# Moving two stages of the attention output's way through memory, splitting a wait, and cutting loads and stores into tiles

## The chip, the cores and the metric

The kernel runs on one core of one Trainium2 chip. The metric is the device time of one execution in microseconds (us); the shorter the better.

## The reference

x has 2 x 1024 tokens of 512 values. Four residual stages follow each other, each of the form x = x + layernorm(f(layernorm(x))):

```
x = x + _layernorm(_L0_attn_ref(_layernorm(x), w_q, w_k, w_v, w_o))   # 32 heads of 16, full softmax
x = x + _layernorm(_L0_ffn_ref(_layernorm(x), gate, up, down))        # gated FFN, integer weights times scales
x = x + _layernorm(_L1_attn_ref(_layernorm(x), Wqkv, Wo))             # 32 query heads, one key/value head, ALiBi, causal
x = x + _layernorm(_L1_ffn_ref(_layernorm(x), W, b, A, B, p_scores))  # linear plus a clamped low-rank term
```

The change touches the two attention stages only: attention, then the product with w_o (or Wo), its layernorm, and the addition to x.

## The kernel before

Each attention stage (one call of `attention`, tiles named with B and C in the first layer, G and H in the second) computes q, k and v, and then goes through 16 iterations of 4 heads each, 8 for each of the two batches. An iteration is two **turns**, one for each half of 512 queries: 32 turns, 0 to 31. A turn is a row of steps, one for each key tile of 128 (8 in the first layer; 4 or 8 in the causal second). TensorE makes scores and the product with v, ScalarE exponentials, VectorE the maxima of the rows for the turns ahead. The maxima of turn t become rows of the q stack (`max_rows(t)` on SyncE, four small DMAs, L694), and TensorE's first step of turn t waits for them.

The output of a turn goes through DRAM, since heads and their sums have to change partitions. The stages, all but the engines' parts issued by SyncE in the order of its program, are: `copy_o` (PSUM to `o_copy`; VectorE L933 in layer one, ScalarE L890 in layer two), `store_turn` (L701, 256 KB), `fetch` (L712 `o_packed` and L715 `o_sums`), `invert` (VectorE L939), `store_inverse` (L722), `spread_inverse` (L730), and `divide` on GpSimd (L820), which multiplies and writes the tile `on` for two turns of the same half at once. So batch 1's first 512 tokens are complete after the fifteenth multiply, `divide(30)`, and its last 512 after the sixteenth, `divide(31)`. In the middle of the kernel `after_rows(t)`, called behind `max_rows(t)`, issues the stages of turns t-3, t-4, t-6 and t-7; the end has a list of its own.

`Output` takes `on` in 16 tiles of 128 tokens: `tile_high` (ScalarE L1148) and `tile_low` (VectorE L1154) split a tile into two parts, `tile_piece` (TensorE, L74 to L76) makes 12 products of 512 columns, then `tile_stats` (VectorE), `tile_root` (GpSimd L1178), `tile_norm` (VectorE L1171) and `tile_add` (GpSimd L1186, into `xt`). Tiles 0 to 3 run inside the last turns (TILES_AHEAD = 4), tiles 4 to 15 behind them. x comes in and goes out in four blocks of four tiles by `Output.load` (L1112) and `Output.sync` (L1120), 1 MB each, with room for two blocks. w_o is loaded in one DMA (L192) in iteration 1, and GpSimd splits it into parts from turn 3 on (L212, L214). Engines run their programs in order, and a wait holds everything behind it on its engine.

## Time and profile before

| | us |
|---|---|
| median of 3 runs (2146.11 to 2153.83) | 2146.65 |
| the profiled execution's own time | 2145.93 |
| its span | 2144.0 |
| TensorE busy | 1921.5 (90%) |
| VectorE busy | 1422.2 (66%) |
| ScalarE busy | 1142.0 (53%) |

Times inside a trace count from the start of the span. The share of TensorE is an average over stages; in the tail of an attention stage it is far lower. The first attention ends and the gated FFN's first load is issued at 949.65, the second ends at 2018.63.

### The profile page before, as it was taken

To read this page: it belongs to the slowest core of one execution; us is meant where nothing else is said; L and a number is where in the kernel's file an instruction comes from. 1 tells how busy PE (TensorE), PEld (TensorE's weight loads), DVE (VectorE), ACT (ScalarE), POOL (GpSimd) and SP (SyncE) were. 2 spreads that over 40 slices of the span, in tenths; PEclk is the share of its full clock that TensorE was granted. 3 is DMA by queue.
4 is the path that set the end of the run, shared out by engine and by line. 5 is a ranking of instruction groups with operands and counts; after the bars stand their busy time and mean duration, and the time that the engine had idled before them with its cause. 6 is when DMAs were issued, how large, how long until landed. Compare 5 with 4: busy or idle time off the path is not lost. (4 is left out here: it accounts for less than half of the span.)

```text
span 2144.0 us, 31834 instructions
## 1 busy us (share of the span) xinstructions
PE 1921.5 (90%) x11664; PEld 1087.6 (51%) x11664; DVE 1422.2 (66%) x2444; ACT 1142.0 (53%) x2391; POOL 211.3 (10%) x251
## 2 busy tenths in 40 slices
PE   5999999999999999659999999499999999996585
PEld 4864333333333333347888887364444444443463
DVE  5346979999999997354433231567777787763577
ACT  3214777888887887313322221125677777763143
POOL 0000010000000000330010010100100000002313
PEclk9999999999999999879999999699999999998798
DMA  6582443354335431243010100462633444412411
GB/s 202 158 190 74 66 105 69 56 84 76 63 65 82 75 57 39 76 165 100 16 40 1 40 20 0 143 162 68 137 77 79 81 87 90 80 54 76 171 41 59
DMA packets 133434, 178.16 MB, mean 83 GB/s; under 512 B 48244, under 2 KB 59380, under 8 KB 133136
## 3 DMA queue, kind: packets, MB, share of 16 engines
q1 hardware_dynamic: 132896, 175.38, 35.4%
q8 instruction: 92, 1.51, 0.3%
q0 software_dynamic: 384, 0.77, 0.1%
q14 instruction: 62, 0.51, 0.1%
HBM read 111.21 MB, written 64.36 MB: 82 GB/s over the span
## 5 line engine op out<-in xcount | busy, mean ns | idle before, releaser
L927 DVE TENSOR_REDUCE maxesB<-banksB 128x1 f32<-128x1024 f32 x512 | 602.2, 1216 | 92.4 <-PE banksB L993 92.3
L883 ACT ACTIVATE probsB<-banksB 128x512 f32<-128x512 f32 x1024 | 529.6, 602 | 134.8 <-PE banksB L1004 134.7
L924 DVE CUSTOM_DVE_ANT_0 junkG<-banksG,rampG 128x896 bf16<-128x896 f32 (+7 forms) x512 | 368.2, 756 | 104.1 <-PE banksG L993 95.5
L1004 PE MATMUL banksB<-q_stackB,k_stackB 50*128 50x512 f32 x1024 | 405.1, 473 | 7.8 <-DMA q_stackB<-mpartsB 4.8
L883 ACT ACTIVATE probsG<-banksG 128x512 f32<-128x512 f32 (+3 forms) x768 | 326.2, 492 | 119.6 <-PE banksG L1015 68.4
L993 PE MATMUL banksB<-k_stackB,q_stackB 48*128 48x512 f32 x1024 | 345.7, 443 | 3.7
L1004 PEld LDWEIGHTS banksB<-q_stackB,k_stackB 50*128 50x128 f32 x1024 | 167.6, 185 | 270.5 <-ACT probsB L883 228.1
L1004 PE MATMUL banksG<-q_stackG,k_stackG 54*128 54x512 f32 (+3 forms) x768 | 259.6, 413 | 22.0 <-ACT probsG L883 16.5
L1037 PE MATMUL banksB<-probsB,v_onesB 128*32 128x512 f32 x2048 | 276.0, 611 | 0.0
L993 PE MATMUL banksG<-k_stackG,q_stackG 52*128 52x512 f32 (+3 forms) x768 | 248.2, 409 | 11.0 <-DVE maxesG L924 8.2
L993 PEld LDWEIGHTS banksB<-k_stackB,q_stackB 48*128 48x128 f32 x1024 | 155.0, 186 | 85.0 <-DVE maxesB L927 73.8
L1004 PEld LDWEIGHTS banksG<-q_stackG,k_stackG 54*128 54x128 f32 x768 | 126.9, 186 | 103.8 <-ACT probsG L883 75.2
L993 PEld LDWEIGHTS banksG<-k_stackG,q_stackG 52*128 52x128 f32 x768 | 126.2, 187 | 96.6 <-DVE maxesG L924 62.8
L1332 DVE SCALAR_TENSOR_TENSOR hD<-u_psD,suD,siluD 128x512 f32<-128x512 f32 (+1 forms) x44 | 33.0, 750 | 202.3 <-PE u_psD L76 199.9
L1037 PE MATMUL banksG<-probsG,v_onesG 128*32 128x512 f32 (+3 forms) x1536 | 165.4, 503 | 0.1
L1015 PE MATMUL banksG<-masks,halves 64*128 64x64 bf16 (+1 forms) x1024 | 119.9, 211 | 0.0
L1292 ACT ACTIVATE siluD<-g_psD,sgD 128x512 f32<-128x512 f32 (+1 forms) x44 | 30.3, 688 | 132.1 <-PE g_psD L76 132.0
L1300 ACT ACTIVATE hhD<-hD 128x512 fp32r<-128x512 f32 (+1 forms) x44 | 27.8, 632 | 118.3 <-DVE hD L1332 118.3
L1037 PEld LDWEIGHTS banksB<-probsB,v_onesB 128*32 128x32 f32 x2048 | 40.4, 108 | 63.7 <-ACT probsB L883 35.1
L74 PE MATMUL g_psD<-xhTD,wg_highD 128*128 128x512 f32 (+1 forms) x176 | 70.3, 399 | 1.4 <-DVE xlTD L171 1.4
L76 PE MATMUL g_psD<-xhTD,wg_lowD 128*128 128x512 f32 (+1 forms) x176 | 70.3, 399 | 0.0
L74 PE MATMUL y_psD<-wd_highD,hhD 128*128 128x512 f32 (+1 forms) x176 | 70.0, 398 | 0.0
(229 smaller groups left out, 2759.5 us busy)
## 6 DMA issues: line engine op xcount, KB each, us to landing
q_stackB<-q_parts SPq DMA_DIRECT2D x96, 128.0 KB, 6.8
k_stackB<-k_parts SPq DMA_DIRECT2D x96, 128.0 KB, 7.2
q_stackG<-q_parts SPq DMA_DIRECT2D x96, 128.0 KB
q_parts<-partsA SPq DMA_DIRECT2D x16, 512.0 KB, 4.2
k_parts<-partsA SPq DMA_DIRECT2D x16, 512.0 KB, 2.8
turns<-o_copyB SPq DMA_DIRECT2D x32, 256.0 KB
q_parts<-partsF SPq DMA_DIRECT2D x16, 512.0 KB, 2.8
turns<-o_copyG SPq DMA_DIRECT2D x32, 256.0 KB, 3.3
```

The costliest lines, as they stand in the source:

```text
L74: pe.matmul(out, left[0], right[0], start=start, stop=False)
L76: return pe.matmul(out, left[1], right[0], start=False, stop=stop)
L883: act.activation(probs[:, (i % ring) * GH + h, first:HALF], st_ps[:, n % n_st, first:HALF], ACT.Exp).then_inc(st_used, 1)
L924: dve.tensor_tensor_reduce(junk[:, n % JUNK, 0:width], scores, ramp[:, SEQ - width:SEQ], 1.0, LOWEST, ALU.add, ALU.max, out).then_inc(maxe ...
L927: dve.reduce_max(out, scores, AX.X).then_inc(maxed, 1)
L993: ins = pe.matmul(s_ps[:, slot_of[n] + part, 0:b - a], qst[at, it % 3, half, h % GS, qt * P:(qt + 1) * P], kst[at, it % 3, h % kh, a:b], s ...
L1004: ins = pe.matmul(st_ps[:, n % n_st, first:HALF], kst[at, it % 3, h % kh, kt * P:(kt + 1) * P], qst[at, it % 3, half, h % GS, first:HALF], ...
L1015: ins = pe.matmul(st_ps[:, n % n_st, first:first + wide], halves[at, a, :], masks[at, a, 0:wide], start=False, stop=a == 1)
L1037: ins = pe.matmul(o_ps[32 * h:32 * h + 32, first:HALF], vone[:, it % 2, kt, h % vh, :], probs[:, (i % ring) * GH + h, first:HALF], start=k ...
L1292: act.activation(silu[0:k, :], g_ps[0:k, :], ACT.Silu, scale=sg[0:k, j:j + 1]).then_inc(silu_out, 1)
L1300: act.activation(hh[0:k, c % 2, :], h[0:k, :], ACT.Copy).then_inc(hh_out, 1)
L1332: dve.scalar_tensor_tensor(out=h[0:k, :], in0=u_ps[0:k, :], scalar=su[0:k, j:j + 1], in1=silu[0:k, :], op0=ALU.mult, op1=ALU.mult).then_in ...
```

## The change

Six edits. (1) `after_rows(t)` issues the stages of turns t-2, t-3, t-4 and t-5 instead of t-3, t-4, t-6 and t-7, and VectorE's `invert` goes with them. (2) The list at the end is written anew: the last turns' stages stand earlier, and `store_turn(31)` comes behind three stores of single tiles instead of behind block 0's store and block 2's load. (3) `tile_high` for block 2 waits for fifteen multiplies, and for block 3 for sixteen (before, both for sixteen); `tile_low(12)` takes the place in the order that `tile_low(8)` had. (4) x is loaded and stored a tile (256 KB) at a time through eight slots, one load in each of the iterations 1 to 8. (5) w_o is loaded in four chunks in iterations 1 to 4, and GpSimd splits them from turn 10 on. (6) `divide(31)` and `invert(31)` stand later among the tiles, the multiplies of turns 26 and 27 earlier.

```
--- before.py
+++ after.py
@@ -191,6 +191,13 @@
         for k, ap in self.aps.items():
             sp.dma_start(self.raw[k][:, :, :], ap.rearrange("(c p) e -> p c e", p=P)).then_inc(self.loaded[k], 16)
+    def load_chunk(self, sp, c):
+        k = self.order[0]
+        if c:
+            sp.wait_ge(self.loaded[k], 16 * c)
+        sp.dma_start(self.raw[k][:, c, :], self.aps[k][P * c:P * (c + 1), :]).then_inc(self.loaded[k], 16)
     def split_high(self, act, keys):
         for k in keys:
             act.wait_ge(self.loaded[k], 16)
@@ -207,8 +214,7 @@
     def split_piece(self, pool, i):
         k = self.order[0]
-        if i == 0:
-            pool.wait_ge(self.loaded[k], 16)
+        pool.wait_ge(self.loaded[k], 16 * (i + 1))
         pool.tensor_copy(self.high[k][:, i, :], self.raw[k][:, i, :]).then_inc(self.high_out, 1)
         pool.wait_ge(self.high_out, i + 1)
         pool.tensor_tensor(self.low[k][:, i, :], self.raw[k][:, i, :], self.high[k][:, i, :].bitcast(F32),
@@ -732,14 +738,14 @@
             def after_rows(t):
-                if 0 <= t - 3 < TURNS:
-                    store_turn(t - 3)
-                if 0 <= t - 4 < TURNS:
-                    fetch(t - 4)
-                if 0 <= t - 6 < TURNS:
-                    store_inverse(t - 6)
-                if 0 <= t - 7 < TURNS:
-                    spread_inverse(t - 7)
+                if t >= 2:
+                    store_turn(t - 2)
+                if t >= 3:
+                    fetch(t - 3)
+                if t >= 4:
+                    store_inverse(t - 4)
+                if t >= 5:
+                    spread_inverse(t - 5)
             def load_more():
                 sp.wait_ge(proj.w.ready, proj.w.total)
@@ -775,29 +781,36 @@
                     load_stacks(sp, it + 2)
                 if it == 1:
                     proj.stored_block(sp, NB - 1)
-                    out.w.load(sp)
-                    out.load(sp, 0)
-                    sp.wait_ge(out.x_loaded, 16)
-                    out.load(sp, 1)
-            store_turn(last - 2)
-            fetch(last - 3)
+                if 1 <= it <= DC:
+                    out.w.load_chunk(sp, it - 1)
+                if 1 <= it <= out.SLOTS:
+                    out.load(sp, it - 1)
             fetch(last - 2)
-            spread_inverse(last - 6)
-            store_inverse(last - 5)
-            spread_inverse(last - 5)
+            spread_inverse(last - 4)
+            store_inverse(last - 3)
             store_turn(last - 1)
+            spread_inverse(last - 3)
             fetch(last - 1)
-            for t in range(last - 4, last):
-                store_inverse(t)
-                spread_inverse(t)
-            out.sync(sp, range(0, 1))
+            store_inverse(last - 2)
+            spread_inverse(last - 2)
+            store_inverse(last - 1)
+            spread_inverse(last - 1)
+            early = max(tiles_ahead - 1, 0)
+            for t in range(early):
+                out.store(sp, t)
             store_turn(last)
             fetch(last)
+            for t in range(early):
+                out.load(sp, out.SLOTS + t)
             store_inverse(last)
             spread_inverse(last)
+            for t in range(early, NT):
+                out.store(sp, t)
+                if early <= t - 1 < NT - out.SLOTS:
+                    out.load(sp, out.SLOTS + t - 1)
             sp.wait_ge(m_rows, n_rows * TURNS)
             sp.wait_ge(i_spread, 16 * TURNS)
-            out.sync(sp, range(1, NB))
+            sp.wait_ge(out.stored, 16 * NT)
         @block.gpsimd
         def _(pool):
@@ -823,8 +836,8 @@
             def after_split(t):
                 if t >= 8 and t // 2 % 2:
                     divide(t - 8)
-                if 3 <= t < 3 + out.w.count("wo"):
-                    out.w.split_piece(pool, t - 3)
+                if 10 <= t < 10 + out.w.count("wo"):
+                    out.w.split_piece(pool, t - 10)
             for dst, src in copies:
                 pool.dma_start(dst, src).then_inc(copied, 16)
@@ -851,12 +864,11 @@
                 if tile_at(i, 2) is not None:
                     out.tile_root(pool, tile_at(i, 2))
                     out.tile_add(pool, tile_at(i, 2))
-                if i == first_of[last] + 5:
-                    divide(last - 5)
-                    divide(last - 4)
+                if i in (first_of[last] + 1, first_of[last] + 3):
+                    divide(last - 5 + (i - first_of[last] - 1) // 2)
             divide(last - 1)
             for t in range(tiles_ahead, NT):
-                if t == tiles_ahead + 2:
+                if t == tiles_ahead + 4:
                     divide(last)
                 out.tile_root(pool, t)
                 out.tile_add(pool, t)
@@ -952,13 +964,12 @@
             for i, (it, half, kt, *_) in enumerate(steps):
                 for n in units_at[i]:
                     maximum(n)
-                if i - 1 == first_of[2 * it + half] and 2 * it + half >= 5:
-                    invert(2 * it + half - 5)
+                if i - 1 == first_of[2 * it + half] and 2 * it + half >= 3:
+                    invert(2 * it + half - 3)
                 if not causal and kt == 0 and i:
                     copy_o(2 * it + half - 1)
-                if i - first_of[last] in (2, 4):
-                    invert(last - 4 + (i - first_of[last] - 2))
-                    invert(last - 3 + (i - first_of[last] - 2))
+                if i - first_of[last] in (3, 5):
+                    invert(last - 2 + (i - first_of[last] - 3) // 2)
                 if tile_at(i, -1) is not None:
                     out.tile_low(dve, tile_at(i, -1))
                 if tile_at(i, 2) is not None:
@@ -969,13 +980,13 @@
                 copy_o(TURNS - 1)
             for t in range(tiles_ahead, NT):
                 out.tile_stats(dve, t, s_ps)
-                if t + 2 < NT and (t + 2) % (NT // BATCH):
+                if t + 2 < NT and t + 2 != NT - TB:
                     out.tile_low(dve, t + 2)
                 if t > tiles_ahead:
                     out.tile_norm(dve, t - 1, s_ps)
-                if t + 2 < NT and (t + 2) % (NT // BATCH) == 0:
+                if t + 2 == NT - TB:
                     out.tile_low(dve, t + 2)
-                if t == tiles_ahead + 1:
+                if t == tiles_ahead + 2:
                     invert(last)
             out.tile_norm(dve, NT - 1, s_ps)
...
+    SLOTS = 8
     def __init__(self, sb, load_sb, sems, tag, x, x_out, wo_ap, power):
         self.x, self.x_out, self.power = x, x_out, power
...
-        self.xt = load_sb(f"xt{tag}", [P, 2, TB, D], F32)
+        self.xt = load_sb(f"xt{tag}", [P, self.SLOTS, D], F32)
...
-    def load(self, sp, nb):
-        sp.dma_start(self.xt[:, nb % 2, :, :], self.x[BLK * nb:BLK * (nb + 1), :].rearrange("(t p) d -> p t d", p=P)
-                     ).then_inc(self.x_loaded, 16)
-    def sync(self, sp, blocks):
-        for nb in blocks:
-            sp.wait_ge(self.added, TB * (nb + 1))
-            if nb:
-                sp.wait_ge(self.stored, 16 * nb)
-            sp.dma_start(self.x_out[BLK * nb:BLK * (nb + 1), :].rearrange("(t p) d -> p t d", p=P), self.xt[:, nb % 2, :, :]
-                         ).then_inc(self.stored, 16)
-            if nb + 2 < NB:
-                sp.wait_ge(self.stored, 16 * (nb + 1))
-                sp.wait_ge(self.x_loaded, 16 * (nb + 2))
-                self.load(sp, nb + 2)
-            if nb == NB - 1:
-                sp.wait_ge(self.stored, 16 * NB)
+    def load(self, sp, t):
+        if t:
+            sp.wait_ge(self.x_loaded, 16 * t)
+        if t >= self.SLOTS:
+            sp.wait_ge(self.stored, 16 * (t - self.SLOTS + 1))
+        sp.dma_start(self.xt[:, t % self.SLOTS, :], self.x[P * t:P * (t + 1), :]).then_inc(self.x_loaded, 16)
+    def store(self, sp, t):
+        sp.wait_ge(self.added, t + 1)
+        if t:
+            sp.wait_ge(self.stored, 16 * t)
+        sp.dma_start(self.x_out[P * t:P * (t + 1), :], self.xt[:, t % self.SLOTS, :]).then_inc(self.stored, 16)
     def tile_piece(self, pe, t, c, y_ps):
@@ -1141,8 +1149,10 @@
     def tile_high(self, act, t, divided, turns):
-        if t % (NT // BATCH) == 0:
-            act.wait_ge(divided, turns * (t // (NT // BATCH) + 1))
+        batch, half = divmod(t // TB, 2)
+        if t % TB == 0:
+            act.wait_ge(divided, turns * (batch + 1) - 1 + half)
         if t >= 3:
             act.wait_ge(self.made, t - 2)
         act.activation(self.onh[:, t % 3, :, :], self.on[:, :, t * P:(t + 1) * P], ACT.Copy).then_inc(self.high_out, 1)
@@ -1180,9 +1190,8 @@
     def tile_add(self, pool, t):
         pool.wait_ge(self.normed, t + 1)
-        if t % TB == 0:
-            pool.wait_ge(self.x_loaded, 16 * (t // TB + 1))
-        x = self.xt[:, t // TB % 2, t % TB, :]
+        pool.wait_ge(self.x_loaded, 16 * (t + 1))
+        x = self.xt[:, t % self.SLOTS, :]
         pool.tensor_tensor(x, x, self.yn[:, t % 2, :], ALU.add).then_inc(self.added, 1)
```

SyncE in the first layer, behind the stacks of iteration 3 (`q_stackB`, `k_stackB`). Before:

```order
L675 DMA q_stackB<-q_parts 16x4x512
L676 DMA k_stackB<-k_parts 16x2x1024
L192 DMA wo_rawC<-in_w_o 128x4x512
L1112 DMA xtC<-in_x 128x4x512 x2
L694 DMA q_stackB<-mpartsB 1x8x128 x4
L684 DMA v_loadB<-v_rows 128x512
```

Now:

```order
L681 DMA q_stackB<-q_parts 16x4x512
L682 DMA k_stackB<-k_parts 16x2x1024
L199 DMA wo_rawC<-in_w_o 128x512
L1129 DMA xtC<-in_x 128x512
L700 DMA q_stackB<-mpartsB 1x8x128 x4
L690 DMA v_loadB<-v_rows 128x512
```

The maxima's rows (L694, now L700) stood behind two loads of 1 MB, of which the second waited for the first; now they stand behind two of 256 KB with no wait between.

SyncE at the end of the first layer's attention, from the last but one inverse's spreading on, with the semaphores waited for. Before:

```order
L730 DMA o_inverseB<-inverses 64x1x512 [waits inverses_spread_1,inverses_stored_1]
L1120 DMA x<-xtC 128x4x512 [waits x_added_C_1]
L1112 DMA xtC<-in_x 128x4x512 [waits x_loaded_C_1,x_stored_C_1]
L701 DMA turns<-o_copyB 128x512 [waits o_stored_1,o_copied_1]
L712 DMA o_packedB<-turns 64x1x512 [waits o_moved_1,sums_moved_1,o_divided_1,o_stored_1]
L715 DMA o_sumsB<-turns 128x1x16 [waits sums_inverted_1]
L722 DMA inverses<-o_recipB 128x16 [waits inverses_stored_1,sums_inverted_1]
```

Now:

```order
L736 DMA o_inverseB<-inverses 64x1x512 [waits inverses_spread_1,inverses_stored_1]
L1135 DMA x<-xtC 128x512 [waits x_added_C_1]
L1135 DMA x<-xtC 128x512 [waits x_stored_C_1,x_added_C_1] x2
L707 DMA turns<-o_copyB 128x512 [waits o_stored_1,o_copied_1]
L718 DMA o_packedB<-turns 64x1x512 [waits o_moved_1,sums_moved_1,o_divided_1,o_stored_1]
L721 DMA o_sumsB<-turns 128x1x16 [waits sums_inverted_1]
L1129 DMA xtC<-in_x 128x512 [waits x_stored_C_1,x_loaded_C_1] x3
L728 DMA inverses<-o_recipB 128x16 [waits inverses_stored_1,sums_inverted_1]
L736 DMA o_inverseB<-inverses 64x1x512 [waits inverses_spread_1,inverses_stored_1]
L1135 DMA x<-xtC 128x512 [waits x_stored_C_1,x_added_C_1] x2
```

The last turn's store no longer follows a 1 MB store and load; three loads of a tile stand between its sums and its inverses, and every store of a tile but the first waits for the one before.

GpSimd at the same place, from tile 3's addition on. Before:

```order
L1186 TENSOR_TENSOR xtC<-xtC,ynC 128x512
L820 TENSOR_TENSOR onC<-o_packedB,o_inverseB 128x512
L1178 TENSOR_TENSOR yrstdC<-ymvC,power 128x1
L1186 TENSOR_TENSOR xtC<-xtC,ynC 128x512
L1178 TENSOR_TENSOR yrstdC<-ymvC,power 128x1
L1186 TENSOR_TENSOR xtC<-xtC,ynC 128x512
L820 TENSOR_TENSOR onC<-o_packedB,o_inverseB 128x512
```

The second L820 is the last turn's multiply, behind tile 5; now it stands behind tile 7, with two more pairs of root and addition ahead of it (its row in the new order, between tiles 7 and 8):

```order
L1195 TENSOR_TENSOR xtC<-xtC,ynC 128x512
L833 TENSOR_TENSOR onC<-o_packedB,o_inverseB 128x512
L1188 TENSOR_TENSOR yrstdC<-ymvC,power 128x1
L1195 TENSOR_TENSOR xtC<-xtC,ynC 128x512
L1188 TENSOR_TENSOR yrstdC<-ymvC,power 128x1
```

## Rows read from the trace of the kernel before

**Rows 1.** PE, timeline, three stretches: start, us, form, idle before and its releaser.

```profile
279.79 0.79 PE L1004 MATMUL banksB<-q_stackB,k_stackB 50*128 50x512 f32 x1 [4.44 <-DMA q_stackB<-mpartsB]
...
911.03 0.79 PE L74 MATMUL banksB<-wo_highC,onhTC 128*128 128x512 f32 x1 [18.72 <-DVE onlTC L1154]
```

**Rows 2.** SyncE, timeline, at the loads of x in iteration 1 of each layer.

```profile
260.74 13.29 SPq L1112 DMA_DIRECT2D xtC<-in_x  x2
...
1510.92 10.45 SPq L1112 DMA_DIRECT2D xtH<-x  x2
```

**Rows 3.** GpSimd, timeline, first layer: w_o's first split, the last turn's multiply.

```profile
271.04 0.62 POOL L212 CAST wo_highC<-wo_rawC 128x512 fp32r<-128x512 f32 x1 [20.87 <-DMA wo_rawC<-in_w_o]
...
908.32 1.26 POOL L820 TENSOR_TENSOR onC<-o_packedB,o_inverseB 128x512 f32<-128x512 f32 x1 [2.62 <-DMA o_inverseB<-inverses]
```

**Rows 4.** VectorE, timeline, first layer: a turn's output copied, one row a turn.

```profile
257.32 0.68 DVE L933 COPY o_copyB<-banksB 128x512 f32<-128x512 f32 x1
...
306.69 0.68 DVE L933 COPY o_copyB<-banksB 128x512 f32<-128x512 f32 x1
...
327.72 0.68 DVE L933 COPY o_copyB<-banksB 128x512 f32<-128x512 f32 x1
```

**Rows 5.** ScalarE, timeline, second layer: outputs of turns 1, 5, 7 and 31 copied.

```profile
1498.08 0.60 ACT L890 ACTIVATE o_copyG<-banksG 128x512 f32<-128x512 f32 x1
...
1561.69 0.60 ACT L890 ACTIVATE o_copyG<-banksG 128x512 f32<-128x512 f32 x1
...
1591.25 0.60 ACT L890 ACTIVATE o_copyG<-banksG 128x512 f32<-128x512 f32 x1
...
1955.09 0.60 ACT L890 ACTIVATE o_copyG<-banksG 128x512 f32<-128x512 f32 x1 [1.18 <-PE banksG L1037]
```

**Rows 6.** SyncE, timeline, both tails: last turn's store, inverses, next stage's load.

```profile
892.31 0.45 SPq L701 DMA_DIRECT2D turns<-o_copyB  x1
...
902.69 0.33 SPq L722 DMA_DIRECT2D inverses<-o_recipB  x1
904.90 0.53 SPq L730 DMA_DIRECT2D o_inverseB<-inverses  x1
...
949.65 0.36 SPq L108 DMA_DIRECT2D xD<-x  x1
...
1962.49 0.46 SPq L701 DMA_DIRECT2D turns<-o_copyG  x1
...
2018.63 0.36 SPq L108 DMA_DIRECT2D xI<-x  x1
```

**Rows 7.** VectorE, timeline, first tail: last copy, tile 7's low part, norms of 8 and 15.

```profile
881.97 0.68 DVE L933 COPY o_copyB<-banksB 128x512 f32<-128x512 f32 x1
...
887.93 0.69 DVE L1154 TENSOR_TENSOR onlTC<-onC,onhTC 128x512 fp32r<-128x512 f32 x1
...
921.12 0.81 DVE L1171 TENSOR_SCALAR ynC<-banksB,ymvC,yrstdC 128x512 f32<-128x512 f32 x1 [0.44 <-POOL yrstdC L1178]
...
941.94 0.81 DVE L1171 TENSOR_SCALAR ynC<-banksB,ymvC,yrstdC 128x512 f32<-128x512 f32 x1 [1.89 <-POOL yrstdC L1178]
```

**Rows 8.** DMA issues of the whole span: count, size, median us to landing.

```profile
v_loadB<-v_rows SPq DMA_DIRECT2D x16, 256.0 KB, 3.0
...
x<-xtH SPq DMA_DIRECT2D x4, 1024.0 KB, 4.3
...
x<-xD SPq DMA_DIRECT2D x4, 256.0 KB, 2.0
```

**Rows 9.** The tile view of turns: landing times of its stores and fetches.

```profile
DMA to landing us min/median/max: 2.0/3.3/5.9
```

**Rows 10.** Timeline, first layer, mid run: sums fetched on SyncE.

```profile
639.84 0.55 SPq L715 DMA_DIRECT2D o_sumsB<-turns  x1
```

**Rows 11.** Timeline, first layer, mid run: VectorE's reciprocal of that turn's slot.

```profile
646.51 0.24 DVE L939 RECIPROCAL o_recipB<-o_sumsB 128x16 f32<-128x16 f32 x1
```

**Rows 12.** Windows: us, busy us by engine, granted clock (PEclk), DMA share, GB/s.

```profile
278.00:282.00 4.00, 2.21 (x9) 1.45 (x10) 0.92 (x1) 1.38 (x3) 0.00 (x0) 0.50 0.61 177
```

## The prediction

> **What bounds the kernel now.** I read the timeline of TensorE first, looking for its long gaps, then the engine behind each gap, then SyncE, whose program order decides both. In the middle of the attention stages TensorE is nearly full; nothing that the change moves can shorten that. Two kinds of place are different, and each occurs once per attention layer.
>
> The first is iteration 1. TensorE waits 4.44 us at 279.79 for the maxima's rows [rows 1], and right after it the granted clock is 0.50, the lower level of 1.2 GHz [rows 12]. The rows came late because SyncE stood between two 1 MB loads of x for 13.29 us, in the second layer 10.45 [rows 2]; GpSimd, which has to split the maximum too, was itself standing before w_o's first split until 271.04 [rows 3]. What it cost in all is read from the copies of a turn's output, one a turn. First layer: 257.32 to 306.69 are two turns in 49.37 us, and the next turn takes 327.72 - 306.69 = 21.03 [rows 4]; 49.37 - 2 x 21.03 = **7.3 us** lost. Second layer: four turns from 1498.08 to 1561.69 in 63.61, two regular ones 29.56 (1561.69 to 1591.25) [rows 5]; 63.61 - 59.12 = **4.5 us** lost.
>
> The second is the tail. TensorE idles 18.72 us before tile 8 at 911.03 [rows 1], since the last turn's output goes through DRAM: its copy starts at 881.97 [rows 7], but SyncE issues the store at 892.31 [rows 6], having stood behind block 0's store and block 2's load; the inverses are spread at 904.90, and GpSimd multiplies at 908.32 [rows 3, 6]. From then on tiles run at VectorE's and GpSimd's pace, tile 8's norm at 921.12 to tile 15's at 941.94: seven steps, 2.97 us each [rows 7]. The next stage's load is issued 949.65 - 941.94 = 7.7 us after that [rows 6, 7].
>
> **The change part by part.**
>
> *Iteration 1.* SyncE no longer waits between loads there, and GpSimd's splits come when the chunks have long landed. SyncE issues two DMAs more in iterations 1 to 4, one more to 8; these stand behind the stacks' loads, ahead of maxima that are not due yet, so I cost them at nothing. With the rows on time TensorE has no gap there and no low clock: both losses go, 7.3 + 4.5 = **11.8 us**. Bounds: 0 (if the rows were late for the traffic's sake) and 11.8.
>
> *Two turns sooner, in mid run.* The same DMAs, so no time by itself. What gets tighter is the reciprocal: its sums are now those that SyncE has fetched in the same turn. The place of the two in a turn stays, and that is 646.51 - 639.84 = 6.7 us from issue to use [rows 10, 11]. Landings of this tile are 2.0 to 5.9, median 3.3 [rows 9]: covered. If not, VectorE stands, with the maxima behind it and TensorE's next turn behind those. At the end the gain is that turns 28 to 30 are through before the last turn ends.
>
> *The tail, first layer.* (a) The last store goes out when the copy is done, 881.97 + 0.68, say 882.7, instead of 892.31: the three tiles' stores ahead of it belong to tiles 0 to 2, done in the turn. (b) It lands after 3.3 [rows 9], the fetches go out at about 886 and 886.6, and three loads of tiles follow, each waiting for the one before: 3.0 us for 256 KB [rows 8], so 887.1, 890.1, 893.1. These hold the inverses' store to 893.5; spread 904.90 - 902.69 = 2.2 later [rows 6], 895.7, and landed 3.4 later (908.32 - 904.90 [rows 3, 6]), 899.1. (c) Meanwhile TensorE makes tiles 4 to 11 without the gap, since turn 30's multiply is done at about 882. Tile 7's low part at 887.93 [rows 7] is followed by tile 4's norm at about 888.7 (before, GpSimd stood in a multiply there). Eleven steps of 2.97 to tile 15 are 32.7; the last turn's multiply adds its 1.3 [rows 3] between tiles 7 and 8, where it no longer waits (tile 7 is added after 899.1); and tile 12's parts, which can only be made behind that multiply and stand behind tile 9's norm, I take at 1 us. So tile 15's norm comes at 888.7 + 32.7 + 1.3 + 1 = 923.7, its addition ends 2.1 later, and by computing alone the last store goes out at **925.9**. TensorE stands up to 4 us before tile 12 and may fall to the lower clock, as it did after 4.44 us [rows 1, 12]; that adds up to 2 here.
>
> (d) But the stores are a chain of their own: 13 of them behind the last spreading, each waiting for the one before. The first, tile 3's, goes out at 896.3. A store of 256 KB lands in 2.0 [rows 8], 2.2 with issue; five of them have a load behind them, and I take 3.3 for such a round (the load's 3.0 and an issue). Twelve steps: 2.3 + 5 x 3.3 + 6 x 2.2 = 32.0, so the last goes out at **928.3**, later than by computing. The stores thus end last, by 2.4 us, and hide a fall of the clock.
>
> (e) The last landing is of 256 KB, 2.0, not of 1 MB, 4.3 [rows 8]. Before, 7.7 lay between tile 15's norm and the next stage; less 2.1 for the norm and the addition and 4.3 for the landing leaves 1.3 for the barrier. So the next stage begins at 928.3 + 2.0 + 1.3 = 931.6 instead of 949.65: **18.1 us**.
>
> *The tail, second layer.* The last copy is at 1955.09, so the store goes out at 1955.8 instead of 1962.49 [rows 5, 6]. That is 1073.1 after the first layer's; with the same chain the next stage begins at 931.6 + 1073.1 = 2004.7 instead of 2018.63 [rows 6]: **13.9 us**.
>
> Sum: 11.8 + 18.1 + 13.9 = 43.8. The profiled execution took 2145.93 (span 2144.0), 0.7 below the median of the runs, so 2145.9 - 43.8 = 2102.1 against the profiled one and 2102.9 against the median; **2103 us**.
>
> **A price that the trace bounds only from far: the chain of small stores.** No stores of 256 KB that wait for each other stand in the trace. The four in the FFN overlap and land in 2.0; the widest landing near is 5.9 [rows 8, 9]. I take 2.2 and 3.3, nearer to the first, since in the tail nothing else moves but the loads. The Trainium skill ("DMA: Bandwidth & Descriptors", section Bandwidth) advises to batch DMAs to 1 MiB or more, which speaks against this edit; its section on the anatomy of a DMA fits a fixed 2.0 us plus bytes at 436 GB/s. By that a tile's store is 2.6 us, twelve steps 31.2, and the total about 1.6 us lower than mine; the trace agrees on the fixed part, since a block of four times the size takes 2.3 us more, not four times as long.
>
> **The rivals.**
>
> *The forecast (72%)*: both holes of iteration 1 go, both tails shorten by 14 to 20 us, stores or computing ending last.
>
> *The chain of stores binds harder (16%)*. For it: SyncE's program has them all behind the last spreading, and landings of 3.3 are the median of a tile of this size beside other traffic [rows 9]. With 4.3 in the five rounds with a load and 3.3 in the seven without, the twelve steps are 44.6 instead of 32.0, 12.6 later in each layer: 2128. Against it: in the tail the queues are nearly empty. Part of the way is likelier than all of it.
>
> *The holes of iteration 1 remain (4%)*, because the stacks' loads and not SyncE's wait make the rows late: only the tails gain, 32.0, and the time is 2115. Against it: the same stacks' loads stand in every iteration, and the regular turns have no such gap.
>
> *Computing binds (5%)*: landings of 2.0 all over and tile 12 never late; each tail 2.4 to 4 us shorter than forecast, 2096.
>
> *Slower (2%)*: the reciprocal waits in mid run. Each turn in which the sums land later than 6.7 us after issue [rows 10, 11] holds VectorE by the difference. To eat 43.8 us over some 58 turns takes 0.75 each, a landing of 7.5; beyond 7.7 the kernel is slower by over 0.5%, and at 8.5 it stands at 2103 + 58 x 1.8 = 2207. Against it: 5.9 is the longest landing seen [rows 9].
>
> *Nothing moves (1%)*: something that the trace does not show releases tile 8 and the maxima's rows.
>
> **How the numbers follow.** Half a per cent, 11 us, is about what a measurement of this kernel can tell from no change. The forecast case spans 2096 to 2109; the range reaches up into the chain of stores half way (2116) and down past the case in which computing binds (2094), which leaves out what is beyond half of that rival and the last two. **Range 2094 to 2116.** Faster by over 0.5% (below 2136): all of the forecast, of computing, of the remaining holes and nearly all of the chain, 96%; within, 2%; slower, 2%.
>
> **What the new profile would show.** Right: no wait of TensorE on `q_stackB<-mpartsB` above a few tenths at 275 to 280, copies of turns 21.0 apart throughout; the last `turns` store within 1 us of the last copy; TensorE's longest gap in the tail before tile 12, some 4 us; 13 stores of `xt` in a row on SyncE, about 2.2 apart and 3.3 with loads; the FFN's first load about 7.3 + 18.1 = 25.4 us earlier, at 924, and the adapter's first load 43.8 earlier, at 1975. Wrong: reciprocals waiting for `o_sums` in mid run, stores more than 4 us apart, additions waiting for x's tiles, or a gap before tile 8.

## The result, and the profile after

The changed kernel takes 2114.5 us (median of 4 runs, 2109.6 to 2119.3) beside 2146.4 for the kernel before on the same chip: ratio 0.985, interval 0.9823 to 0.9877. The forecast was 2103 and the range 2094 to 2116, so the direction is right and the median lies near the upper end. The profiled execution took 2118.06, with a span of 2116.2; it is 3.6 above the median, so a part of what its stretches show belongs to this one execution.

The span splits into stretches between rows that stand in both traces (turn copies, and the next stage's first load):

| stretch | before | after | difference | forecast |
|---|---|---|---|---|
| start to turn 0's copy, layer one | 215.26 | 214.47 | -0.8 | 0 |
| turn 0's to turn 31's copy, layer one | 666.71 | 669.83 | **+3.1** | -7.3 |
| tail, layer one | 67.68 | 47.93 | **-19.75** | -18.1 |
| gated FFN and projection | 528.44 | 529.88 | +1.4 | 0 |
| turn 0's to turn 31's copy, layer two | 477.00 | 476.24 | -0.8 | -4.5 |
| tail, layer two | 63.54 | 48.65 | **-14.9** | -13.9 |
| adapter stage | 125.4 | 129.2 | +3.8 | 0 |

The tails gave what was forecast and a little more. In the first layer, turns behind iteration 1 took back more than iteration 1 gave. TensorE's timeline of the changed kernel shows where (it answers to [rows 1]):

```profile
318.72 0.50 PE L1015 MATMUL banksB<-q_stackB,k_stackB 50*128 50x512 f32 x1 [1.96 <-DMA q_stackB<-mpartsB]
...
407.60 0.50 PE L1015 MATMUL banksB<-q_stackB,k_stackB 50*128 50x512 f32 x1 [1.68 <-DMA q_stackB<-mpartsB]
...
909.57 0.50 PE L74 MATMUL banksB<-wo_highC,onhTC 128*128 128x512 f32 x1 [2.78 <-DVE onlTC L1164]
```

The wait at 279.79 is gone, but the same releaser, the maxima's rows, now holds TensorE twice, with the rows that SyncE issues in its iterations 2 and 4. VectorE's copies of turns 4 and 5 (as in [rows 4]) and the last one:

```profile
298.73 0.68 DVE L945 COPY o_copyB<-banksB 128x512 f32<-128x512 f32 x1
322.63 0.69 DVE L945 COPY o_copyB<-banksB 128x512 f32<-128x512 f32 x1 [0.74 <-PE banksB L1048]
...
884.30 0.69 DVE L945 COPY o_copyB<-banksB 128x512 f32<-128x512 f32 x1 [1.84 <-PE banksB L1048]
```

This turn took 322.63 - 298.73 = 23.90 instead of 21.04. The eight turns to the copy of turn 12 lose 9.8 us in all. SyncE's timeline, from the last stack load of iteration 2 on:

```profile
304.41 0.59 SPq L682 DMA_DIRECT2D k_stackB<-k_parts  x1
305.04 0.42 SPq L199 DMA_DIRECT2D wo_rawC<-in_w_o  x1
305.50 0.43 SPq L1129 DMA_DIRECT2D xtC<-in_x  x1
311.93 2.79 SPq L700 DMA_DIRECT2D q_stackB<-mpartsB  x4
```

SyncE is free and issues the rows at 311.93, 21 us after the last ones (290.89): nothing on SyncE is late. The windows (columns as in [rows 12]) show what is:

```profile
302.00:306.00 4.00, 4.00 (x28) 1.29 (x26) 3.76 (x4) 3.46 (x7) 0.00 (x0) 1.00 1.06 117
306.00:310.00 4.00, 4.00 (x28) 1.66 (x24) 3.50 (x4) 2.92 (x7) 0.00 (x0) 1.00 1.08 125
310.00:314.00 4.00, 4.00 (x28) 1.39 (x27) 3.56 (x4) 3.69 (x9) 0.45 (x1) 1.00 1.05 124
...
320.00:324.00 4.00, 4.00 (x18) 1.57 (x17) 2.79 (x4) 2.01 (x5) 0.61 (x1) 0.50 0.12 39
```

The DMA engines are full (share 1.05 to 1.08) from 302 to 314, at only 117 to 125 GB/s, and the rows stand behind that. Behind the late rows the granted clock falls to 0.50 (1.2 GHz). The waits before these two rows are 3.6 us of the 9.8, so the turns behind them lose more than the waits. The kernel before had the same full stretch behind its stacks, without these loads, and then a gap before its rows, which it issued at 319.90:

```profile
314.00:318.00 4.00, 4.00 (x28) 1.70 (x24) 3.50 (x4) 2.92 (x7) 0.00 (x0) 1.00 1.00 116
318.00:322.00 4.00, 4.00 (x27) 1.36 (x27) 3.56 (x4) 3.69 (x9) 1.80 (x3) 1.00 0.12 19
```

In the tail, SyncE (as [rows 6]), then VectorE's statistics of tile 12, its last norm, and GpSimd's last addition:

```profile
885.02 0.32 SPq L707 DMA_DIRECT2D turns<-o_copyB  x1
...
888.26 7.19 SPq L1129 DMA_DIRECT2D xtC<-in_x  x3
895.64 0.33 SPq L728 DMA_DIRECT2D inverses<-o_recipB  x1
898.06 0.54 SPq L736 DMA_DIRECT2D o_inverseB<-inverses  x1
...
915.01 14.21 SPq L1135 DMA_DIRECT2D x<-xtC  x7
...
932.23 0.37 SPq L108 DMA_DIRECT2D xD<-x  x1
```

```profile
914.22 0.70 DVE L1169 BATCH_NORM_STATS2 ystatsC<-banksB 128x6 f32<-128x512 f32 x1 [1.77 <-PE banksB L76]
...
926.73 0.81 DVE L1181 TENSOR_SCALAR ynC<-banksB,ymvC,yrstdC 128x512 f32<-128x512 f32 x1 [1.88 <-POOL yrstdC L1188]
```

```profile
927.62 1.26 POOL L1195 TENSOR_TENSOR xtC<-xtC,ynC 128x512 f32<-128x512 f32 x1 [0.92 <-DVE ynC L1181]
```

The last addition ends at 928.88, and the seventh store of the last row is issued at 915.01 + 14.21 - 0.32 = 928.90, as soon as its tile is there; in the second layer the two times are 1983.10 and 1983.13. So computing ends last and not the chain of stores, but in the first layer only just. A narrower window shows the store before the last alone:

```profile
926.71 0.32 SPq L1135 DMA_DIRECT2D x<-xtC  x1
```

Tile 14's addition had ended at 926.19, so this store still waited for the one before it. Stores that wait only for each other stand 2.06 apart here (922.59, 924.64, 926.71), and by that the chain alone would have reached the last store at 928.8, an estimate, 0.1 us before the addition's end. TensorE's wait of 2.78 us at 909.57 reaches the tail: the clock behind it is 0.57 in the mean,

```profile
910.00:914.00 4.00, 4.00 (x12) 3.15 (x11) 1.94 (x5) 0.00 (x0) 3.08 (x4) 0.57 0.66 222
```

and VectorE waits 1.77 us for tile 12's product at 914.22.

### The profile page after: what moved, and what is told of

Same layout as the page of the kernel before. It is cut to its first block and busy times, and to the rows that moved or that the text cites. A ratio compares the mean times of both kernels' runs of the same rounds, so it can differ in the third digit from the quotient of the medians.

```text
span 2116.2 us, 31952 instructions
## 1 busy us (share of the span) xinstructions
PE 1929.8 (91%) x11664; PEld 1092.3 (52%) x11664; DVE 1420.7 (67%) x2444; ACT 1141.4 (54%) x2391; POOL 211.2 (10%) x251
## 5 line engine op out<-in xcount | busy, mean ns | idle before, releaser
L826 POOL TENSOR_TENSOR mpartsB<-mrowB,mpartsB 16x128 fp32r<-16x128 f32 x32 | 14.4, 451 | 571.6 <-ACT mrowB L885 571.6
```

## The experiments

Three groups: what makes turns long in mid run (e1, e2, e3, e4), what the parts of the tail are worth (e3, e6, e7), and what bounds the tail now (e5, e8, e9, e10). The profiled execution of each is cut as in the table above; ratios are to the kernel before on the same chip.

**e1_idle.** The loads of iterations 1 to 8 move from behind the stacks to behind the even turn's stages, ahead of a stretch in which the DMA engines have nothing to do (share 0.00 from 324 to 334):

```
                 if 2 * it not in early_turns:
                     after_rows(2 * it)
+                if it == 1:
+                    proj.stored_block(sp, NB - 1)
+                if 1 <= it <= DC:
+                    out.w.load_chunk(sp, it - 1)
+                if 1 <= it <= out.SLOTS:
+                    out.load(sp, it - 1)
```

> The changed kernel, with the loads of iterations 1 to 8 (a chunk of w_o and a tile of x) issued behind the stages of the even turn instead of behind the stacks. Theory (the loads share the DMA engines with the stacks and make the maxima's rows late): in the first layer the 318.72 and 407.60 waits for q_stackB<-mpartsB go and so does the low clock behind them, the copies of turns 4 to 12 are 21.04 to 21.1 apart, and the time from turn 0's copy to turn 31's falls from 669.8 by 8 to 10 us to about 660; the second layer by 0 to 4; ratio to before 0.9805, about 2105 us. Rival (the shift of the stages by two turns or the clock by itself makes the long turns): the long turns stay at 23 to 24 us, the ratio stays at 0.985.

Measured: 2102.85 us, ratio 0.9771 (0.9744 to 0.9799). Copies 4 to 11 are 21.02 to 21.05 apart, first to last copy 661.8 (was 669.8), second layer 472.4 (was 476.2), tails unchanged (47.3 and 48.7). The same windows of this kernel:

```profile
306.00:310.00 4.00, 4.00 (x28) 1.66 (x24) 3.51 (x4) 2.93 (x7) 0.00 (x0) 1.00 1.07 125
310.00:314.00 4.00, 4.00 (x28) 1.39 (x27) 3.56 (x4) 3.69 (x9) 0.45 (x1) 1.00 0.34 46
```

The rows are again issued at 311.93, but now the engines have just come free (0.34). Later there is one wait of 0.81 us for rows at 739.47, with no load of x near: the stacks alone leave hardly any slack. The ratio fell by more than these 8.0 us, by 17 from 0.985. The spans differ by 3.9 in the second layer's turns and by 4.5 in the FFN and the adapter, which the edit doesn't touch. The same edit between e5 and e8, on one chip, takes the median from 2109.0 to 2101.0: 8.0 us is what it is worth.

**e2_apart.** x's tiles are loaded in iterations 5 to 12, so 256 KB an iteration instead of 512:

```
-                if 1 <= it <= out.SLOTS:
-                    out.load(sp, it - 1)
+                if DC < it <= DC + out.SLOTS:
+                    out.load(sp, it - 1 - DC)
```

> The changed kernel, with the tiles of x loaded in iterations 5 to 12 instead of 1 to 8, so that behind the stacks of iterations 1 to 4 stand 256 KB instead of 512. Theory (DMA engines are full behind the stacks): the two waits for the maxima's rows shrink from 1.96 and 1.68 us to a few tenths or nothing, turns 4 to 12 lose under 2 us instead of about 9, and the time is 2107 us. Rival (stage shift or clock): turns as long as before the edit, 2114 us. If already 256 KB more were too much, iterations 5 to 12 would show holes too.

Measured: 2109.7 us, ratio 0.9807 (0.9779 to 0.9835). Turns 4 to 12 lose 0.2 us, but later turns, with the x tiles, lose some 4 in all, with this wait behind the second of those tiles:

```profile
485.07 0.50 PE L1015 MATMUL banksB<-q_stackB,k_stackB 50*128 50x512 f32 x1 [1.10 <-DMA q_stackB<-mpartsB]
```

So 256 KB behind the stacks is at the edge: nothing in iterations 1 to 4, then now and then 1 us with its low clock.

**e3_lags.** The stages' shift by two turns is undone, with the old list at the end and the old places of the reciprocals and multiplies there:

```
-                if t >= 2:
-                    store_turn(t - 2)
-                if t >= 3:
-                    fetch(t - 3)
+                if t >= 3:
+                    store_turn(t - 3)
+                if t >= 4:
+                    fetch(t - 4)
...
-                if i - 1 == first_of[2 * it + half] and 2 * it + half >= 3:
-                    invert(2 * it + half - 3)
+                if i - 1 == first_of[2 * it + half] and 2 * it + half >= 5:
+                    invert(2 * it + half - 5)
```

> The changed kernel, with the stages of a turn's output issued as before the change (for turns t-3, t-4, t-6 and t-7, the reciprocal five turns behind) and the old order of the last turns' stages; loads by tile and chunk, the split wait and the tail stay. Theory (extra loads behind the stacks): the waits of 1.96 and 1.68 us and the long turns stay, 670 us from the first to the last copy of layer one; the tail of layer one is up to 3 us longer, since turns 28 to 30 come later; about 2116 us. Rival (the shift by two turns makes the rows late): the long turns go, about 661 us from copy to copy, and the time is about 2107.

Measured: 2127.1 us, ratio 0.9884 (0.9858 to 0.991). Long turns stay, though not the same ones, with 670.1 from copy to copy and a wait of 1.91 at 361.70, so the shift doesn't cause them. The tails are 56.4 and 55.4, longer by 8.5 and 6.7 where I expected up to 3. SyncE:

```profile
883.93 0.41 SPq L728 DMA_DIRECT2D inverses<-o_recipB  x1
887.18 0.53 SPq L736 DMA_DIRECT2D o_inverseB<-inverses  x1
887.77 6.79 SPq L1138 DMA_DIRECT2D x<-xtC  x3
894.65 0.38 SPq L707 DMA_DIRECT2D turns<-o_copyB  x1
```

The last copy is at 884.60, but the last turn's store goes out ten us later: the old list's inverses and the three stores behind them are still being issued. The shift and the new list together clear SyncE before the last turn ends; no run parts the two.

**e4_wait.** SyncE waits again, with the traffic unchanged:

```
                 if 1 <= it <= out.SLOTS:
                     out.load(sp, it - 1)
+                if it == 1:
+                    sp.wait_ge(out.x_loaded, 16)
```

> The changed kernel, and SyncE waits in iteration 1 for the first tile of x to land (same traffic, only SyncE's wait is back). Theory (a wait of SyncE holds the rows behind it): the landing took 12.4 us in the first layer, rows that were issued at about 269.9 go out at about 273.7 to 276, TensorE waits 2 to 6 us at about 278 and falls to the lower clock, so the first layer is 3 to 7 us longer than the changed kernel's; in the second layer 0 to 4; in all 2118 to 2124 us. Rival (the traffic alone made the hole of iteration 1 before the change, and SyncE's wait cost nothing): no hole there and 2114 us.

Measured: 2123.0 us, ratio 0.987 (0.9838 to 0.9902). The rows go out at 273.69, and TensorE stands:

```profile
277.65 0.79 PE L1017 MATMUL banksB<-q_stackB,k_stackB 50*128 50x512 f32 x1 [2.46 <-DMA q_stackB<-mpartsB]
```

The second layer's hole is back as well: a wait of 2.51 at 1520.62 and one turn of 24.30 instead of 19.98 (24.15 in the kernel before). First to last copy is 673.8 and 478.8, 4.0 and 2.6 above the changed kernel. The two turns to the copy of turn 4 lose 5.8 us, where they lost 7.3 before the change. So SyncE's wait alone makes most of the old hole, as the prediction had it, and the traffic behind the stacks is a second cause. A further 3.0 us of this run lie in the FFN and projection, which the edit doesn't touch.

**e5_order.** In the tail, the loads of tiles 8 to 10 come behind the inverses' spreading, the last reciprocal and multiply one tile sooner, tile 12's low part ahead of tile 9's norm:

```
             store_inverse(last)
             spread_inverse(last)
             for t in range(early, NT):
+                if t - early < NT - out.SLOTS:
+                    out.load(sp, out.SLOTS + t - early)
                 out.store(sp, t)
...
-                if t == tiles_ahead + 4:
+                if t == tiles_ahead + 3:
                     divide(last)
```

> The changed kernel with the tail in another order: the loads of tiles 8 to 10 come behind the inverses' spreading, one ahead of each store, the last reciprocal and the last multiply stand one tile sooner, and tile 12's low part ahead of tile 9's norm. Theory (computing ends last, and TensorE's wait before tile 12 with the low clock behind it is what delays it): the wait of 2.78 us at 909.57 shrinks to below 1 us, the last store comes 3 to 4 us sooner after the last copy in each layer (tails of 47.9 and 48.7 us become about 44.5 and 45), the kernel is 6 to 8 us faster than the changed one: ratio to before 0.982 where the changed one had 0.985. Rival (the chain of stores ends last, as the prediction had it): the loads now stand among the stores, the tails stay at 48 us or grow by up to 3, ratio 0.985 to 0.988.

Measured: 2109.0 us, ratio 0.9818 (0.9799 to 0.9837), which is not told apart from 0.985. TensorE's wait before tile 12 halves to 1.38 us, yet the tails are 47.6 and 48.1, only 0.4 and 0.5 shorter. The theory misses. The rival has the tails' number (48) but not the cause: the last store goes out at 927.76, as the last addition ends (927.73). GpSimd's timeline shows what sets the pace:

```profile
912.01 1.30 POOL L1191 TENSOR_TENSOR xtC<-xtC,ynC 128x512 f32<-128x512 f32 x1 [0.93 <-DVE ynC L1177]
913.27 0.99 POOL L1184 TENSOR_TENSOR yrstdC<-ymvC,power 128x1 f32<-128x1 f32 x1
915.19 1.29 POOL L1191 TENSOR_TENSOR xtC<-xtC,ynC 128x512 f32<-128x512 f32 x1 [0.93 <-DVE ynC L1177]
...
921.08 1.26 POOL L1191 TENSOR_TENSOR xtC<-xtC,ynC 128x512 f32<-128x512 f32 x1 [0.93 <-DVE ynC L1177]
922.30 0.55 POOL L1184 TENSOR_TENSOR yrstdC<-ymvC,power 128x1 f32<-128x1 f32 x1
923.77 1.26 POOL L1191 TENSOR_TENSOR xtC<-xtC,ynC 128x512 f32<-128x512 f32 x1 [0.92 <-DVE ynC L1177]
```

Norm, addition and the next tile's root follow each other round: 0.9 + 1.3 + 1.0 = 3.18 us a tile while VectorE still makes low parts, 2.69 once it makes none. What the smaller wait gives is lost here: VectorE no longer waits 1.77 us, but the rounds of tiles 8 to 12 are 3.16 to 3.18, where the changed kernel has some of 2.70 to 2.78. From tile 4's norm to tile 15's it is 34.8 us, and 35.2 in the changed kernel.

**e6_blocks.** The last twelve tiles are stored as three blocks of 1 MB:

```
-            for t in range(early, NT):
-                out.store(sp, t)
-                if early <= t - 1 < NT - out.SLOTS:
-                    out.load(sp, out.SLOTS + t - 1)
+            out.store(sp, early)
+            out.load(sp, out.SLOTS + early)
+            for nb in range(1, NB):
+                out.store_block(sp, nb)
...
```

> The changed kernel, with the last twelve tiles of x stored in three DMAs of 1 MB behind each other instead of twelve of 256 KB. Theory (computing ends last; the small stores only make the last landing short): each tail is 2 to 2.5 us longer than the changed kernel's (a block lands in 4.3 us, a tile in 2.0 to 2.3), 4 to 5 us in all, ratio to before 0.987. Rival (the chain of small stores ends last): tails 0 to 2 us shorter, ratio 0.984 to 0.985.

Measured: 2113.1 us, ratio 0.9848 (0.9826 to 0.9871). The total can't tell it from the changed kernel, but the tails are 50.2 and 50.7, 2.3 and 2.0 longer, the difference of the last landing: the last store goes out 44.6 us after the last copy in both kernels, with three stores as with twelve, so the chain of small stores doesn't lengthen the changed kernel's tail. SyncE:

```profile
914.14 11.23 SPq L1144 DMA_DIRECT2D x<-xtC  x2
930.61 0.36 SPq L108 DMA_DIRECT2D xD<-x  x1
```

From the last store's issue (925.00) to the next load are 5.6 us; the changed kernel has 3.3. The Trainium skill ("DMA: Bandwidth & Descriptors", section Bandwidth) advises 1 MiB or more to a DMA. This case differs for the store that ends a stage: there the landing of 1 MB costs the 2.3 us more.

**e7_whole.** Block 2 waits for all sixteen multiplies, with the order of before around it:

```
-            act.wait_ge(divided, turns * (batch + 1) - 1 + half)
+            act.wait_ge(divided, turns * (batch + 1) if batch else turns)
```

> The changed kernel, with block 2 waiting for all sixteen multiplies again, and the order of tile 8's and tile 12's low parts, the last reciprocal and the last multiply as before the change. Theory (the split wait removes the gap before tile 8): TensorE stands before tile 8 from about 898 to 905 in the first layer, 7 to 9 us, falls to the lower clock, and each tail is 6 to 9 us longer than the changed kernel's: 12 to 18 us in all, about 2130 us. Rival (the earlier store of the last turn alone makes the gain): each tail within 3 us of the changed kernel's, about 2118 us.

Measured: 2134.0 us, ratio 0.9929 (0.9907 to 0.9951). The tails are 55.6 and 56.2, longer by 7.7 and 7.5, and the gap is back:

```profile
908.99 0.80 PE L74 MATMUL banksB<-wo_highC,onhTC 128*128 128x512 f32 x1 [8.90 <-DVE onlTC L1164]
```

**e8_best.** The edits of e1_idle and e5_order together.

> Both edits together: the loads of iterations 1 to 8 behind the even turn's stages (2102.85 us when alone), and the tail's new order. If the two are independent, the gain of the tail's order adds: 6 to 8 us less, 2095 to 2097 us, ratio to before 0.974; with the chain of stores as the bound in the tails 2103 us, ratio 0.977.

Measured: 2101.0 us, ratio 0.9784 (0.9761 to 0.9807), tails 47.5 and 48.1, copies of layer one all within 21.00 to 21.07 until the last two. The forecast of 2095 to 2097 for two gains that add is missed: the loads give 8 us (against e5), and the order nothing that can be measured (against e1).

**e9_roots.** As e8_best, and in the tail the next tile's root stands ahead of the addition:

```
+                if t == tiles_ahead:
+                    out.tile_root(pool, t)
+                if t + 1 < NT:
+                    out.tile_root(pool, t + 1)
...
-                out.tile_root(pool, t)
                 out.tile_add(pool, t)
```

> The kernel with both edits (loads of iterations 1 to 8 behind the even turn's stages, tail in the new order), and in the tail GpSimd makes the root of tile t+1 ahead of the addition of tile t instead of behind it. Theory (in the tail a ring of VectorE's norm, GpSimd's addition and GpSimd's next root sets the pace: 0.89 + 1.25 + 1.00 = 3.18 us a tile, and TensorE's wait before tile 12 was only filled by it): norms come 2.7 to 2.8 us apart, at TensorE's and VectorE's pace, and by computing alone each tail is 4 to 5 us shorter, 43.5 instead of 47.5 and 44 instead of 48.1. But the stores wait for each other, 2.7 us apart with a load between and 2.5 without, so if that chain ends last now the tails are only 1 to 2 us shorter. Rival (DMA latency and the last multiply set the tail already): tails unchanged within 0.5 us. Time 2092 us by computing, 2098 us by the chain, 2101 us by the rival.

Measured: 2100.3 us (2092.7 to 2102.6), ratio 0.9778 (0.9755 to 0.9801). Norms are mostly 2.64 to 2.72 apart (3.49 at the last turn's multiply), TensorE has no gap of 1 us, and the tails are 45.4 and 45.7, 2.1 and 2.4 shorter than in e8. GpSimd's last two additions, and SyncE's last stores:

```profile
908.49 2.48 POOL L1194 TENSOR_TENSOR xtC<-xtC,ynC 128x512 f32<-128x512 f32 x2 [0.20 <-DVE ynC L1180]
```

```profile
905.00 11.01 SPq L1134 DMA_DIRECT2D x<-xtC  x6
919.00 0.37 SPq L108 DMA_DIRECT2D xD<-x  x1
```

The additions end at 910.97, but the last store goes out at 915.69: now the chain of small stores ends last, by 4.7 us. Its last five stores, with no load between, are 2.06 apart. That is the forecast's second case, of tails only 1 to 2 us shorter, and a little better.

**e10_pairs.** As e9_roots, with tiles 4 to 13 stored in pairs:

```
+            PAIRS = ((3, 4), (4, 6), (6, 8), (8, 10), (10, 12), (12, 14), (14, 15), (15, 16))
+            for k, (a, b) in enumerate(PAIRS):
...
+                out.store(sp, a, b, early + k)
```

> The kernel e9_roots, and tiles 4 to 13 are stored in pairs of 512 KB (five stores instead of ten), tiles 3, 14 and 15 alone. Theory (with the ring gone the chain of stores ends last): stores no longer lag behind the additions, and the tails are 2 to 3 us shorter than in e9_roots, 43.5 and 44 us. Rival (computing ends last in e9_roots too): tails as in e9_roots within 0.5 us.

Measured: 2094.4 us (2087.7 to 2106.8), ratio 0.9752 (0.9725 to 0.9779). The tails are 44.2 and 43.2, 1.3 and 2.5 shorter than in e9_roots, where 2 to 3 were expected:

```profile
905.83 9.37 SPq L1136 DMA_DIRECT2D x<-xtC  x4
918.36 0.37 SPq L108 DMA_DIRECT2D xD<-x  x1
```

The last addition ends at 911.58 and the last store goes out at 914.88, so in the first layer the stores still end last, by 3.3 us instead of 4.7. In these traces it is the shortest pair of tails; the intervals of e8, e9 and e10 overlap, so that the steps between them rest on the tails and not on the totals. Against the changed kernel's 0.985 the last is faster: its interval lies below.

## Why the prediction was right, and where it was wrong

**Iteration 1** (11.8 forecast): the mechanism was right. The wait at 279.79 is gone, the turns there are 21.06, and e4 brings a hole back in both layers with SyncE's wait alone. Both layers' gains are there: 7.3 in the first, and no hole in the second.

**The step that failed** is in the same paragraph: "SyncE issues two DMAs more in iterations 1 to 4, one more to 8; these stand behind the stacks' loads, ahead of maxima that are not due yet, so I cost them at nothing." I asked when SyncE would be free, and it was. I did not ask when the DMA engines would be. They work on the stacks until about 311 (e1), and the rows are issued at 311.93, so that there was no cover for 4 us of further traffic (an estimate: 512 KB at 117 to 125 GB/s). It was in the trace of before: a DMA share of 1.00 at 314 to 318, behind a set of stacks, and rows at 319.90. It cost 9.8 us in turns 4 to 12, of which the two waits are 3.6; the rest falls in turns that begin at the lower clock. e1 moves the loads and has 8.0 back in the first layer. The rival "the holes of iteration 1 remain", which I gave 4%, has the time that came (2115), but that is a coincidence: its holes of iteration 1 are gone, and e4 shows that SyncE's wait made them. It looked at the right queue, though. My argument against it, that regular turns with the same stacks have no gap, left out that they have no load behind the stacks either.

**The range held partly by luck.** Its upper end, 2116, was set for a chain of stores half way to its rival. The stores took less than forecast, and what filled the room was the term that I had at nothing: without the 9.8 us the profiled execution would be near 2108, inside the forecast case of 2096 to 2109.

**Two turns sooner** (nothing in mid run): right: a single reciprocal waits for its sums, 0.24 us at 259.81. But the worth of the shift and the new list at the end, which the prediction had only inside the tail's sum, is large: 8.5 and 6.7 us (e3).

**The tail** (18.1 and 13.9): 19.75 and 14.9. By steps, counted from the start of the last copy: inverses stored 11.5 later by forecast, 11.3 measured; tile 15's norm 41.7 and 42.4; last store 46.3 by the chain of stores, 44.6 measured, and 43.9 by computing; then 3.3 to the next stage in both. So the sizes held, but "the stores thus end last" was wrong: the twelve steps took 30.2 us and not 32.0. The first was longer, 4.2 instead of 2.3; the five with a load behind them took 2.1 to 2.8 instead of 3.3; the last seven stores took 13.9, 2.3 apart, where one with no load costs 2.06 by itself. Computing thus ends last, by about 0.1 us in the first layer and 0.6 in the second (both estimates from the 2.06). Its pace is mostly the ring of norm, addition and root: e9 shows that by breaking it, in the order of e8. In the changed kernel's own order nobody broke it, and with stores so close behind little could be gained there; TensorE's wait before tile 12 has a share in the pace that no run parts from the ring. The case "computing binds" had 5% and was the one here, though without its never-late tile 12, and by 1.7 and 1.0 us a tail instead of 2.4 to 4. The prediction's sentence on the fixed part of a DMA reads too much into the trace: 2.0 us for 256 KB and 4.3 for 1 MB give a fixed part of 1.2 (an estimate); no term of the sum uses it. The parts nearly add: 8.5 (e3) + 7.7 (e7) + 2.3 (e6) = 18.5 of 19.75, and 6.7 + 7.5 + 2.0 = 16.2 of 14.9.

**What the sum lacked.** The profiled execution is 16.0 above the forecast: 10.4 in the first layer's turns, 3.7 in the second's, 3.8 in the adapter, 1.4 in the FFN, less 2.6 in the tails and 0.8 at the start. The median is 11.6 above its forecast of 2102.9. The second layer lost its hole, but three turns there took 21.37 instead of 19.98. The adapter shows two stretches of 4 to 5 us at the lower clock, near 2045 and 2072, that the trace of before lacks. Both come and go from trace to trace: e1 and e9 have no such turn, and the adapter is 125.4 to 126.2 in all ten experiments, which keep most of the change. I have no cause for them, and take them to be no part of the change; since each kernel has one trace, that isn't shown.

## What to carry to other kernels

A load that no engine waits for still has a price, if it is queued ahead of something small that is due soon: look for the stretch in which the DMA engines are idle, and issue it there. When a wait is taken out of a queue's program, check the resource behind the queue as well as the queue's program. In a tail of many small steps, write down the ring of engines that hand the tile to each other; a gap of the matrix engine beside it may be mostly slack, and halving it gave 0.4 to 0.5 us here as long as the ring stood.

## What the hardware showed that I had not expected

The stacks' loads, to 16 partitions each, fill the DMA engines' time (share 1.07) at 125 GB/s in e1, where nothing else is behind them at 306 to 310. The changed kernel's 256 KB tiles in the tail, from 904 to 914, move at 215 to 222 GB/s with a share of 0.62 to 0.66.

The root on GpSimd, 128 x 1 values, takes 0.55 us alone and 0.99 to 1.00 beside VectorE's low part, and that low part takes 0.98 instead of 0.69. The Trainium skill ("SBUF — State Buffer", section Who interferes with whom) says that a VectorE instruction with two inputs in SBUF contends with a GpSimd instruction that reads SBUF; the low part is such an instruction, and the trace agrees, as in e5, where the root at 913.27 takes 0.99 beside it:

```profile
912.87 0.99 DVE L1160 TENSOR_TENSOR onlTC<-onC,onhTC 128x512 fp32r<-128x512 f32 x1
```

It is half a microsecond of each round of the ring.

Behind a wait of 1.96 us TensorE was granted the lower clock: 320 to 324 has 0.50 (1.2 GHz), and the turn lost 2.86 us, 0.9 more than the wait; the next turn lost 1.79 without a wait for rows.
